# Before the fourth expert layer: a front of 12 pages, tables and sums moved, attention outputs added and normed half by half

## The reference

```python
x = x + 0.5 * _L1_ffn_ref(_layernorm(x, axis=-1), ...)
x = x + _L1_attn_ref(_layernorm(x, axis=-1), ...)
x = x + 0.5 * _L1_ffn_ref(_layernorm(x, axis=-1), ...)

# _L1_attn_ref: a linear attention, per sequence of 1024 tokens
    QKV = jnp.einsum('bsd,ed->bse', X, W_in) + b_in
    Q, K = rope(Q, rot_dim), rope(K, rot_dim)
    A = jnp.sum(feature_map(K) * V, axis=-2)      # one row per sequence
    Y = jnp.einsum('bsd,ed->bse', A[:, None, :] * Q, W_out) + b_out
    return Y + X
# _L1_ffn_ref
    scores = jax.nn.sigmoid(x @ gate_w); topk_w, topk_i = jax.lax.top_k(scores, TOP_K)
    # routed: over the 6 experts, combine * ((silu(x wg) * (x wu)) wd); and a shared expert beside it
```

## Time and profile before

| what | us |
|---|---|
| median of 3 runs | 1301.58 (1299.71 to 1303.45) |
| the profiled execution | 1301.21 |
| its span, first to last instruction | 1299.4 |

### The profile page before, as it was taken

The page is one execution under the profiler, slowest core; times in us unless marked ns, Lnnn a source line. Parts: engine busy times, 40 slices in busy tenths (PEclk is TensorE's granted clock), DMA queues, the critical chain, the costliest instruction groups (busy, mean ns, idle before and its releaser), DMA issues. The chain is left out here.

```text
span 1299.4 us, 20577 instructions
## 1 busy us (share of the span) xinstructions
PE 1110.7 (85%) x6035; PEld 918.2 (71%) x6035; DVE 746.4 (57%) x2345; ACT 536.0 (41%) x1012; POOL 594.8 (46%) x579
## 2 busy tenths in 40 slices
PE   4899997887898999988687899999968674899994
PEld 3777775566677887766565799988545553899994
DVE  4663365645635574366645564777788655545554
ACT  3423344464533432244441344444242324466663
POOL 3580244221213233237767303667536777017776
PEclk9799998999988999999888999999888887899998
DMA  9623535920000236534353767887302232569997
GB/s 315 281 94 90 154 102 166 323 98 1 1 1 33 87 141 257 201 120 144 127 198 129 234 209 218 282 252 226 92 8 81 102 106 101 176 205 285 295 288 239
DMA packets 126073, 209.84 MB, mean 161 GB/s; under 512 B 16064, under 2 KB 105536, under 8 KB 124096
## 3 DMA queue, kind: packets, MB, share of 16 engines
q1 hardware_dynamic: 101392, 141.38, 32.8%
q0 software_dynamic: 24576, 67.14, 16.6%
HBM read 129.29 MB, written 101.19 MB: 177 GB/s over the span
## 5 line engine op out<-in xcount | busy, mean ns | idle before, releaser
L713 POOL DMA_INDIRECT G<-yd,slot_of x256 | 251.1, 981 | 297.9 <-DMA yd<-yo 216.4
L698 POOL DMA_INDIRECT xd<-xnt,slot_of x256 | 251.6, 983 | 152.4 <-issue 78.7
L982 PE MATMUL ps<-WE,xT 128*128 x1016 | 190.0, 331 | 0.6 <-issue 0.2
L2210 DVE TENSOR_TENSOR hid<-hid,ps 128x192 f32<-128x192 f32 (+2 forms) x168 | 65.3, 389 | 180.9 <-ACT hid L1624 180.6
L982 PEld LDWEIGHTS ps<-WE,xT 128*128 128x128 f32 x1016 | 164.7, 193 | 2.7 <-issue 2.6
L2189 DVE SCALAR_TENSOR_TENSOR XT<-G,wt,XT 128x256 f32<-128x256 f32 x256 | 127.6, 503 | 62.1 <-DMA G<-yd,slot_of 52.9
L1595 ACT ACTIVATE xT<-ps 128x512 f32<-128x512 f32 (+1 forms) x168 | 99.0, 589 | 140.4 <-PE ps L949 134.6
L1624 ACT ACTIVATE hid<-ps 128x192 f32<-128x192 f32 (+2 forms) x168 | 60.3, 359 | 164.3 <-PE ps L982 164.3
L949 PE MATMUL ps<-ident,xd_in 128*128 128x128 f32 x664 | 102.5, 276 | 29.7 <-DMA xd_in<-xd 20.7
L949 PEld LDWEIGHTS ps<-ident,xd_in 128*128 128x128 f32 x664 | 81.5, 142 | 42.9 <-issue 23.3
L1452 ACT ACTIVATE S<-ps 128x512 f32<-128x512 f32 (+1 forms) x72 | 42.6, 592 | 159.7 <-PE ps L887 157.4
(11 more groups left out here) (265 smaller groups left out, 2168.4 us busy)
## 6 DMA issues: line engine op xcount, KB each, us to landing
xd_in<-xd SPq DMA_DIRECT2D x140, 256.0 KB
yd<-yo SPq DMA_DIRECT2D x140, 256.0 KB, 3.2
WE<-w SPq DMA_DIRECT2D x8, 1280.0 KB, 10.2
xd_in<-xd SPq DMA_DIRECT2D x52, 128.0 KB, 2.3
yd<-yo SPq DMA_DIRECT2D x52, 128.0 KB, 2.0
W0E<-w0e SPq DMA_DIRECT2D x1, 4864.0 KB, 33.3
xd<-xnt,slot_of POOLq DMA_INDIRECT x256, 2.4
G<-yd,slot_of POOLq DMA_INDIRECT x256, 4.1
```

The lines of the kernel that those rows point to most:

```text
L698: nc.gpsimd.indirect_dma_start(xd[f // 2][:, :], bass.IndirectOffsetOnAxis(ap=slot_of[:, t, k:k + 1], axis=0), xnt[:, t, :], None).then_in ...
L713: nc.gpsimd.indirect_dma_start(G[:, n % G_RING, :], None, yd[f // 2][0:min(ly.upto[t][k], ly.TILES) * P, :], bass.IndirectOffsetOnAxis(ap= ...
L982: last = mm(dst, xT[:, q % 2, a, k, :], flat[:, bass.ds(expert[2 * q + a] + k * 2 * ly.H, 2 * ly.H)], start=(k == 0), stop=(k == KD - 1))
L2210: tt(hid[:, q % 2, 0:m, 0:ly.H], hid[:, q % 2, 0:m, 0:ly.H], src, ALU.mult).then_inc(TL.hid, 1)
```

## The change

In layer 2's loop: the front is 12 pages instead of 16; the tables are loaded behind pair 12's load instead of pair 3's; VectorE adds two gathers in each pair, with no third; the norm of blocks 0 and 1 and their residual sums stand at other pairs, and that of block 2 has left the loop for the window, where ScalarE makes its root. In the window: the key sums stand ahead of the rotation of q1 (and `TAKEN` counts so); `project_out` waits for the first block's queries only at first, and puts its parts into banks 0, 4, 1 and 2; VectorE adds a part and takes the statistics of its two tiles at once (`summed`), with block 3's statistics behind block 0's; ScalarE makes block 3's rows behind block 0's scores; `turn` takes tile by tile; GpSimd's sum for block 3 stands behind block 0's scatters.

```diff
 LAYER = [LY[0], LY[0], LY[1], LY[1]]
-FRONT = [0, 0, 16, 0]
...
 WCOL = {"k1": 0, "k2": 1, "q1": 2, "q2": 3, "v1": 4, "v2": 5}
-TAKEN = {"k1": 3, "v1": 4, "v2": 5, "q1": 8, "rn": 10}
...
         TX, TGU, THT, TY = 0, 1, 3, 7
...
             def attention_weights(i):
-                if i == 3:
...
                 gather(2, t)
-                if t in (4, 8, 12):
-                    inverse(AT_NORM, (t - 4) // 4)
-            for b in (2, 3):
-                residual(b)
-            for b in range(NB):
+                if t in (5, 9):
+                    inverse(AT_NORM, (t - 5) // 4)
+            residual(2)
+            scatter(3, 0)
+            residual(3)
+            for b in range(1, NB):
...
             def turn(norm, b, src, bank):
-                pe.wait_ge(norm.rows, NT * (b + 1))
-                for k in range(KD):
-                    for a in range(NT):
+                for a in range(NT):
+                    pe.wait_ge(norm.rows, NT * b + a + 1)
+                    for k in range(KD):
...
                     elif s:
-                        pe.wait_ge(A1.add, n + 1)
+                        pe.wait_ge(A1.add, (1, 3, 4, 4)[n])
...
                 pe.wait_ge(A1.wo, s + 1)
-                pe.wait_ge(A1.qrot, 2 * s + 2)
-                pe.wait_ge(A1.q2, 2 * s + 2)
                 for h in range(ST // 2):
+                    if h % 2 == 0:
+                        pe.wait_ge(A1.qrot, 2 * s + 1 + h // 2)
+                        pe.wait_ge(A1.q2, 2 * s + 1 + h // 2)
                     for i in range(2):
                         a = ((2 * h + i) % NT) * P
-                        dst = ps[:, h, i * D:(i + 1) * D]
+                        dst = ps[:, OUT_BANK[h], i * D:(i + 1) * D]
                         for k in range(KD):
...
             def first_turns(i):
-                if i == 47:
+                if i == 50:
                     turn(AT_NORM, 0, xnt, B_BANK)
-                if i == 57:
+                if i == 61:
                     pe.wait_ge(AT_NORM.hi, 1)
                     turn(AT_NORM, 1, xnt, B_BANK)
...
                 next_turn(0)
+                logits_of(0)
                 attend(1, 1, 2)
-                logits_of(0)
                 attend(1, 2, 3)
                 next_turn(1)
...
             def first_turns(i):
-                if i == 43:
+                if i == 47:
                     rows(AT_NORM, 0, XT[:, tiles_of(0), :])
-                if i == 49:
+                if i == 52:
                     flipped(0, B_BANK)
-                if i == 54:
+                if i == 59:
                     rows(AT_NORM, 1, XT[:, tiles_of(1), :])
-                if i == 59:
+                if i == 63:
                     flipped(1, B_BANK)
...
             def window():
                 chunks = [ch for b in range(NB) for ch in RUN["s", 3, b][0]]
+                keys(0)
+                std(AT_NORM, 2)
                 rows(AT_NORM, 2, XT[:, tiles_of(2), :])
-                keys(0)
                 key_rows(1)
                 key_squares(1)
                 key_root(1)
                 key_query(1)
-                std(AT_NORM, 3)
-                rows(AT_NORM, 3, XT[:, tiles_of(3), :])
                 flipped(2, B_BANK)
                 std(F_NORM[3], 0)
                 rows(F_NORM[3], 0, XT[:, tiles_of(0), :])
-                std(F_NORM[3], 1)
+                std(AT_NORM, 3)
                 plain(0)
                 split_high(0)
+                std(F_NORM[3], 1)
                 score(3, 0, A_BANK + 1)
+                rows(AT_NORM, 3, XT[:, tiles_of(3), :])
                 rows(F_NORM[3], 1, XT[:, tiles_of(1), :])
...
-                    for _ in range(per_pair + (1 if FRONT[f] and (q - q0) % 4 == 3 else 0)):
+                    for _ in range(per_pair):
...
             def key_sums(g):
                 A1.ready(dve, g, "rn")
-                dve.wait_ge(A1.taken, TAKES * g + TAKEN["q1"])
+                dve.wait_ge(A1.taken, TAKES * g + TAKEN["v2"])
...
-                dve.wait_ge(A1.taken, TAKES * (g + 1))
+                dve.wait_ge(A1.taken, TAKES * g + TAKEN["rn"])
...
             def added(s, h):
                 rows = XT[:, s * ST + 2 * h:s * ST + 2 * h + 2, :].rearrange("p t d -> p (t d)")
                 dve.wait_ge(A1.y, 4 * s + h + 1)
-                tt(rows, rows, ps[:, h, :], ALU.add).then_inc(A1.add, 1)
+                tt(rows, rows, ps[:, OUT_BANK[h], :], ALU.add).then_inc(A1.add, 1)
+
+            def summed(b):
+                s = b // 2
+                for i in range(2):
+                    h = 2 * (b % 2) + i
+                    added(s, h)
+                    dve.wait_ge(A1.add, 4 * s + h + 1)
+                    for a in (2 * i, 2 * i + 1):
+                        last = nc.vector.bn_stats(st6[:, a, :], XT[:, b * NT + a, :])
+                st.do(last)
+                st.sync()
+                for a in range(NT):
+                    last = nc.vector.bn_aggr(mv[:, b * NT + a, :], st6[:, a, :])
+                st.do(last)
+                st.sync()
+                ts(rs[:, 0, tiles_of(b)], mv[:, tiles_of(b), 1], EPS, None, ALU.add).then_inc(F_NORM[3].var, 1)
...
             def first_turns(i):
                 NG = LY[1].NG
-                if i in (40, 51, 62):
-                    b = (i - 40) // 11
+                if i in (41, 53):
+                    b = (i - 41) // 12
                     dve.wait_ge(g_used, GATHER0[2] + (b + 1) * NG)
                     stats(AT_NORM, b, XT[:, tiles_of(b), :])
-                if i in (42, 53, 63):
-                    offsets(AT_NORM, (i - 42) // 10)
+                if i in (46, 58):
+                    offsets(AT_NORM, (i - 46) // 12)
                 if i == 50:
                     dve.wait_ge(att_in, 16 * 6)
                     residual(0)
-                if i == 58:
+                if i == 61:
                     residual(1)
...
                 rotated(0, "k1", KB[:, 0, 0, :], A1.krot)
-                gathers(2)
+                gathers(3 * NG - m[0])
+                dve.wait_ge(g_used, GATHER0[2] + 3 * NG)
+                stats(AT_NORM, 2, XT[:, tiles_of(2), :])
                 key_values(0)
                 key_inverse(0)
+                gathers(2)
+                offsets(AT_NORM, 2, True)
+                key_sums(0)
                 rotated(0, "q1", QT[:, 0, 0, :], A1.qrot)
-                key_sums(0)
-                gathers(2)
+                gathers(4)
                 rotated(1, "k1", KB[:, 1, 0, :], A1.krot)
-                gathers(4)
+                gathers(6)
                 key_values(1)
                 key_inverse(1)
-                gathers(4 * NG - m[0])
-                rotated(1, "q1", QT[:, 1, 0, :], A1.qrot)
+                gathers(4)
                 key_sums(1)
                 weighted()
+                rotated(1, "q1", QT[:, 1, 0, :], A1.qrot)
+                gathers(4 * NG - m[0])
+                summed(0)
+                offsets(F_NORM[f], 0, True)
                 last_stats()
                 offsets(AT_NORM, 3, True)
-                added(0, 0)
-                added(0, 1)
-                dve.wait_ge(A1.add, 2)
-                stats(F_NORM[f], 0, XT[:, tiles_of(0), :])
-                added(0, 2)
-                offsets(F_NORM[f], 0, True)
-                added(0, 3)
-                dve.wait_ge(A1.add, 4)
-                stats(F_NORM[f], 1, XT[:, tiles_of(1), :])
+                summed(1)
                 offsets(F_NORM[f], 1, True)
                 rotated(2, "k1", KB[:, 0, 0, :], A1.krot)
...
                 key_inverse(2)
+                key_sums(2)
                 rotated(2, "q1", QT[:, 0, 0, :], A1.qrot)
-                key_sums(2)
...
-                rotated(3, "q1", QT[:, 1, 0, :], A1.qrot)
                 key_sums(3)
                 weighted()
+                rotated(3, "q1", QT[:, 1, 0, :], A1.qrot)
                 dve.wait_ge(A1.res, 2)
-                added(1, 0)
-                added(1, 1)
-                dve.wait_ge(A1.add, 6)
-                stats(F_NORM[f], 2, XT[:, tiles_of(2), :])
-                added(1, 2)
+                summed(2)
                 offsets(F_NORM[f], 2, True)
-                added(1, 3)
-                dve.wait_ge(A1.add, 8)
-                stats(F_NORM[f], 3, XT[:, tiles_of(3), :])
+                summed(3)
...
-            m = tiles(2, 2, 5, first_turns)
+            m = tiles(2, 2, 7, first_turns)
```

More of the change, by code:

```diff
@@ L63 @@
 LAYER = [LY[0], LY[0], LY[1], LY[1]]
-FRONT = [0, 0, 16, 0]
+FRONT = [0, 0, 12, 0]
 EARLY = [LAYER[f].early(FRONT[f]) for f in range(4)]
@@ L83 @@
 WCOL = {"k1": 0, "k2": 1, "q1": 2, "q2": 3, "v1": 4, "v2": 5}
-TAKEN = {"k1": 3, "v1": 4, "v2": 5, "q1": 8, "rn": 10}
+TAKEN = {"k1": 3, "v1": 4, "v2": 5, "rn": 7, "q1": 10}
 TAKES = 10
@@ L321, in program @@
         TX, TGU, THT, TY = 0, 1, 3, 7
+        OUT_BANK = (0, A_BANK, 1, 2)
         def twofold(f, q):
@@ L645, in attention_weights @@
             def attention_weights(i):
```

(2 more changed lines are left out.)

## The result

The changed kernel takes 1307.56 us (median of 11 runs, 1301.57 to 1309.96) against 1301.58 in as many runs of the kernel before; the ratio is 1.0052, 95% interval 1.0037 to 1.0067, which is 4.8 to 8.7 us more. The forecast was +5.3, 1306.5.

What follows compares the result with a forecast made beforehand. GpSimd's 96 gapless scatters fix the end, which moves with the first scatter plus anything put between them. Loop -3.3, window +3.8 and between the scatters +4.85 made +5.3 on the profiled 1301.21: 1306.5 us, range 1298 to 1311.

Steps and rivals of the forecast that it cites:

- The front of 12: Third layer's loop: pair 6 becomes first to wait for block 3's scatters, transposed at 736.5; +4.0 us, bounds +1.5 to +6.
- The tables: Loop, pair 12: 2.2 MB queued ahead of pair 13's load, with four pairs already loaded; +0.2 us, at most 3.
- VectorE's waits in the loop: TensorE's 5.6 us of waits for `hid` shrink as VectorE's work leaves the loop, 1.4 staying for `residual(1)`; -4.2 us.
- The clock at the end: Loop's end: without the last pause, last products save 1.5 us and the first key set 1.8 at full clock; -3.3.
- K: Start of the window's first rotation on VectorE, 917.72 before; forecast to come 3.3 us sooner, at 914.4.
- The window: From the first rotation on VectorE to block 0's `slot_of`: 66.5 us instead of 62.7, +3.8.
- The hold: Window: GpSimd's sum for block 2 stretches two of VectorE's last eight gather additions to 4.84 us instead of 1.0.
- The rival without a hold: Window: GpSimd's block 2 sum and the last gathers miss each other; window 62.8 us, total +1.5, 1302.7; chance 0.2.
- Between the scatters: GpSimd's block 3 sum, now behind 24 of 96 gapless scatters, adds its full time; +4.85 us.
- By WSH: Window: outputs behind the scaled weights, not VectorE's queue, decide the first scatter; total -4.7 us, 1296.5; chance 0.2.
- The loop gives nothing: Loop: new pauses replace the old and hold the clock down, window starts at 917.7; total +8.6, 1309.8; chance 0.15.
- both pauses: Loop: TensorE's new waits at pair 13 behind the tables and at `residual(1)`, replacing the old and lowering the clock.

Runs made afterwards that it cites:

- tables_apart: Changed kernel with the six tables issued one every second pair from pair 12 to 22 instead of all at pair 12; 1.0025 of the kernel before.
- tables_at3: Changed kernel with the tables loaded in one burst at pair 3 again instead of pair 12; 1.0039 of the kernel before.
- sums_vector: Changed kernel with the residual sums of blocks 2 and 3 moved from GpSimd to VectorE, behind set 2's key inverse; 0.9986 of the kernel before.
- front16: Changed kernel with the front of 16 pages back and VectorE's additions six pairs behind instead of seven; 1.0031 of the kernel before.
- sum3_first: Changed kernel with GpSimd's sum for block 3 in front of block 0's scatters again; 1.0029 of the kernel before.
- before_sum3: Kernel before with one edit, GpSimd's sum for block 3 behind block 0's 24 scatters; 1.0034 of the kernel before.
- keysums_late: Changed kernel with the key sums behind the q1 rotations again for the four sets, `TAKEN` as before; 1.0036 of the kernel before.
- block3_behind: Changed kernel with block 3's statistics and norm behind block 0's slots, ScalarE's root and rows behind block 1's rows; 1.0094 of the kernel before.

## Why the prediction was right, and what in it was wrong

The total and its sign were right, but not every term. The clock at the loop's end and the hole between the scatters were met within 0.3, the front within its bounds; the window was 1.9 too small; the tables and VectorE's waits were mis-sized by 3.1 and 4.3 in opposite directions, and that they nearly cancelled is luck.

**The front of 12, +4.0.** Pair 6 was the first to wait, as forecast, but at 732.78 and not 736.5: the last scatter came 14.84 after the loop's start where I had 18.5. That is luck of this execution. Over the five profiles with this front and the tables in one burst the last scatter comes at 18.1 and pair 8 at 32.0; the two with the old loop have 27.0 there: +5.1.

**The tables, +0.2, at most 3: the step that failed.** I had set the burst against the time of four loaded pairs and let it fit. It did not: pair 13 waited 1.80 (757.08) and the pair behind it ran at the lower clock, pair 12 to pair 14 took 9.79 instead of 5.65. That is 4.1 in the profile and 3.3 over the five, above my bound of 3; tables_apart takes it back. The gain I saw, scatters no longer slowed, was real and is of the same size (tables_at3).

**VectorE's waits in the loop, -4.2: mis-sized.** I counted the waits for `hid` alone, 5.6. From pair 14 to pair 62 the kernel before takes 144.49 us and the changed one 136.48, of which 0.87 is a `turn` that moved behind. The 7.1 that are left are three waits for `hid` (3.5 of the 5.6), two for `xT` (0.99 and 1.08), which ScalarE copied behind four rows of the norm that had waited for VectorE's offsets, and 1.5 that the pairs around these waits take beyond the idle that is counted. The clock has no part in it: it was 1.00 from 880 to 892. With the last wait (2.12, now 0.71 in two) it is -8.5. `residual(1)` cost 0.7, not 1.4.

**The clock at the end, -3.3.** From the last product's start to K 3.52 us instead of 6.57: -3.05.

Sum over the profiles: 5.1 + 3.3 - 8.5 - 3.05 = -3.2, against -3.3; K stands 201.4 after the loop's start on average, before 204.6. (The first two are from means, the others from one profile of each kernel.) The profile alone has -6.2.

**The window, +3.8.** Measured +5.7. Up to `WSH` VectorE had the order that I walked down, with additions of 0.56 for my 0.52; but it waited 2.04 for TensorE's second set and not the 0.6 for which I had shown no row. That set took 5.38 us where the first took 3.68, at a granted clock of 0.62 from 935 to 939. This wait goes by where the clock falls: with the same steps up to there it was 0.35 in sums_vector (1.00 from 935 to 941) and 3.73 in front16 (0.50 from 929 to 935). The hold came as priced, 3.9 for 3.8, but not where I put it: one victim was the last step of the rotation (946.26, 2.58 for 0.69), the other the first of the eight additions (948.88, 2.46 for 0.48). From the last addition to `slot_of` 24.4 us, forecast 24.6.

The rival without a hold (62.8) is out. The rule on which I leaned, that GpSimd shares its SBUF interfaces with VectorE (the Trainium skill, GPSIMD Engine Reference, Key points), agrees with this. The Trainium skill (SBUF — State Buffer, Who interferes with whom) says more: the shared pair is locked for a whole instruction, and the one that comes second blocks until the first is through. The traces agree on the lock: the held steps in the kernel before, the changed kernel and sum3_first end 0.02 to 0.6 us behind the end of a step of GpSimd's, and GpSimd's second one took 2.69 for 2.35 where VectorE had come in between. Who comes second isn't told by the starts alone: in sum3_first an addition that starts 0.23 ahead of GpSimd's step (949.88) was held too, 2.87 for 0.48.

**Between the scatters, +4.85.** Measured 4.65, and 4.4 by itself (before_sum3).

**The total.** With the loop's mean the terms make -3.2 + 5.7 + 4.65 = +7.1, with the loop of the profiled execution +4.1; the medians differ by 6.0. The last scatter of layer 2 and the 95 steps vary by as much from one execution to another, so the terms are known no better.

**The rivals.** By WSH: out; VectorE waited for no output. `WSH` came 2.6 sooner after K than before, and the first scatter 5.7 later; in keysums_late, with `WSH` 0.8 later, the first scatter was 1.8 sooner. The loop gives nothing: out, though both pauses that it named came.

## What to carry to other kernels

Price an elementwise step on GpSimd by what VectorE does beside it: a pair of them of 4.85 us cost 3.9 beside additions with both inputs in SBUF, 1.8 beside the routing's small steps and 0.2 where VectorE waited and worked out of PSUM. So put it there, or give it to VectorE in a wait (8.6 us here, with the hole). A wait of TensorE can cost more than its length, when the pairs behind it run at the lower clock (4.1 for 1.80 here), but need not (front16): look at the granted clock behind it. A burst of loads ahead of a stream that is only four pairs deep is better spread, one load every second pair: of the four kernels that had it so, one still waited, 1.54 us.

## What the runs showed of the hardware

- Of VectorE's steps beside GpSimd's sum, elementwise steps with two inputs from SBUF (128x256 and 128x512) and `TENSOR_SCALAR` were held, the latter down to 128x4 (0.72 for 0.17); three `MAX8` of 128x40 (0.39), `RECIPROCAL` of 128x4 (0.18) and an addition out of PSUM (0.69, 959.73 in the earlier trace rows) ran at their usual length.
- The length of an idle time alone did not tell TensorE's clock behind it. Behind pair 13's wait the next 5 us had a mean of 0.66 for 1.80 us (changed), 2.13 (keysums_late) and 1.30 (block3_behind), and 1.00 for 1.32 (sum3_first) and 2.62 (front16).
- Between two scatters that else stand 1.27 apart GpSimd stood idle 4.29 us, for 0.30, when 2.2 MB of tables had just been issued (tables_at3). Without that, the 95 steps of layer 3 still took 120.3 to 123.3 us from one profile to another (the hole left out, and block3_behind, where GpSimd waited for slots), by single steps that are 0.1 to 0.5 longer.
